# Value products of a retention kernel gathered into one stretch per batch

## What is computed

```
xn = layernorm(x)
x  = x + retention(xn; Wq, Wk, Wv, Wo) + ffn(xn)

retention, 8 heads of 16, chunk by chunk of the sequence:
    attn    = (q_c @ k_c.T) * D                 # D: decay below the diagonal
    o_intra = attn @ v_c
    o_inter = (q_c * decay_q) @ S
    S       = decay_s * S + (k_c * decay_k).T @ v_c
    o       = o_intra + o_inter                 # then o @ Wo

ffn:
    h = bitlinear(xn, w_fc) + gate * (xn @ v.T @ fast_b.T @ u.T)
    r = max(h, 0)
    out = bitlinear(r * r, w_proj)              # ternary weights times a row scale
```

## Time and profile before

| | before |
|---|---|
| three executions, us | 179.24, 181.82, 179.17 |
| span of the profiled execution, us | 177.4 |
| TensorE busy, us | 157.6 |
| VectorE busy, us | 137.3 |
| ScalarE busy, us | 78.8 |
| GpSimd busy, us | 61.0 |

### The profile page before, as it was taken

One profiled execution on the slowest core, in us unless ns is written; L12 is line 12 of the kernel. 1 busy time (PEld: TensorE's weight loads), 2 busy tenths in 40 slices (PEclk: granted clock), 3 DMA queues, 4 the chain that ended last, 5 costly groups with the idle time before them and its releaser, 6 DMA issues.

```text
span 177.4 us, 3389 instructions
## 1 busy us (share of the span) xinstructions
PE 157.6 (89%) x1177; PEld 122.1 (69%) x1177; DVE 137.3 (77%) x343; ACT 78.8 (44%) x155; POOL 61.0 (34%) x46
## 2 busy tenths in 40 slices
PE   1561298799999999999999999999999999999992
PEld 0240295577887788787878787878787877788771
DVE  6889898789867988788768876887789757764551
ACT  2510276471277316732583238423762177217710
POOL 8699700065005600380019000920074005500550
PEclk9999999999999999999999999999999999999998
DMA  4970041205240333024301521061005210431001
GB/s 156 431 299 0 0 64 56 59 4 81 37 124 0 60 60 118 0 43 75 114 5 26 92 73 45 7 104 60 6 0 89 33 59 0 74 48 61 0 4 59
DMA packets 7913, 11.65 MB, mean 66 GB/s; under 512 B 1296, under 2 KB 5520, under 8 KB 7776
## 3 DMA queue, kind: packets, MB, share of 16 engines
q1 hardware_dynamic: 7584, 10.82, 25.4%
q10 hardware_dynamic: 320, 0.72, 1.2%
HBM read 5.50 MB, written 2.10 MB: 43 GB/s over the span
## 4 chain that ended last, share of the span: by engine, by line
PE 81%; DVE 13%; DMA 2%; issue 1%; ACT 1%; DVEq 0%
PE ps_o L696 10%; PE ps_score L634 10%; PE ps_score L636 8%; PE ps_score L635 8%; PE ps_work L635 6%; PE ps_work L634 6%; PE ps_work L636 6%; PE ps_y L706 4%; PE ps_y L708 4%; DVE q_dec L453 4%; PE ps_o L685 4%; PE ps_state L688 3%; PE ps_work L656 3%; PE ps_work L630 2%; DMA x_in<-x_tok 2%; PE ps_work L657 2%
## 5 line engine op out<-in xcount | busy, mean ns | idle before, releaser
L301 POOL TENSOR_TENSOR sq_lo<-square,sq_hi 128x512 fp32r<-128x512 f32 x32 | 42.4, 1347 | 107.5 <-ACT sq_hi L369 106.7
L481 DVE TENSOR_TENSOR scores<-ps_score,cst 128x512 f32<-128x512 f32 x64 | 43.8, 686 | 12.6 <-PE ps_score L636 12.5
L365 ACT ACTIVATE square<-ps_work 128x512 f32<-128x512 f32 x32 | 19.0, 599 | 36.3 <-PE ps_work L636 35.6
L634 PE MATMUL ps_score<-q_exp,k_hi 128*128 128x512 f32 x64 | 28.3, 441 | 1.7 <-DVE scores L481 1.7
L636 PE MATMUL ps_score<-q_exp,k_lo 128*128 128x512 f32 x64 | 25.2, 394 | 0.0
L635 PE MATMUL ps_score<-q_exp,k_hi 128*128 128x512 f32 x64 | 25.1, 392 | 0.0
L696 PE MATMUL ps_o<-scores,v_pad 128*32 128x128 f32 x512 | 20.6, 279 | 0.0
L373 ACT ACTIVATE square<-square 128x512 f32<-128x512 f32 x32 | 19.2, 628 | 0.0
L369 ACT ACTIVATE sq_hi<-square 128x512 fp32r<-128x512 f32 x32 | 18.2, 621 | 0.0
L696 PEld LDWEIGHTS ps_o<-scores,v_pad 128*32 128x32 f32 x512 | 12.0, 109 | 7.7 <-issue 5.8
L634 PEld LDWEIGHTS ps_score<-q_exp,k_hi 128*128 128x128 f32 x64 | 12.1, 188 | 6.3 <-issue 3.0
(11 more groups left out here) (94 smaller groups left out, 315.8 us busy)
## 6 DMA issues: line engine op xcount, KB each, us to landing
q_exp<-q_parts SPq DMA_DIRECT2D x60, 64.0 KB, 2.3
x_in<-x_tok SPq DMA_DIRECT2D x8, 256.0 KB, 3.0
resid<-x_feat SPq DMA_DIRECT2D x1, 2048.0 KB, 10.8
out_feat<-resid SPq DMA_DIRECT2D x8, 256.0 KB, 2.1
ffn_in<-ffn_weights SPq DMA_DIRECT2D x1, 576.0 KB, 4.8
cst<-const ACTq DMA_DIRECT2D x1, 468.0 KB, 6.2
wqkv<-qkv_weights ACTq DMA_DIRECT2D x1, 192.0 KB, 5.1
rank_in<-rank_weights ACTq DMA_DIRECT2D x1, 41.1 KB, 2.8
```

Source lines behind the costliest of these rows:

```text
L301: nc.gpsimd.tensor_tensor(sq_lo[:, f, :], square[:, f, :], sq_hi[:, f, :].bitcast(F32), ALU.subtract).then_inc(lo_ready, 1)
L365: nc.scalar.activation(square[:, f, :], ps_work[f % 2][:], ACT.Relu).then_inc(relu_ready, 1)
L481: nc.vector.tensor_tensor(scores[c % 2][:, half * HALF:(half + 1) * HALF], ps_score[half][:].rearrange("p (h i) -> p h i", h=HALF), causal ...
L634: mm(out, w_hi, x_hi, start=True, stop=False)
```

## The change

The value products of the four chunks leave their four places and become one stretch of 32 matmuls, between `project_vk(nxt, 1)` and `second_product`. Its one wait is for all eight masks of the batch. The scores get four buffers, one per chunk. Only the state's product of chunk 1, now the first to write `ps_o` in a batch, carries the start flag; all others add or, where nothing was written since, overwrite.

```diff
-        scores = [sb(f"scores{p}", [P, H, CH]) for p in range(2)]
+        scores = [sb(f"scores{c}", [P, H, CH]) for c in range(NT)]
...
-                    scores[c % 2][:, half * HALF:(half + 1) * HALF],
+                    scores[c][:, half * HALF:(half + 1) * HALF],
...
-                       q_dec[b.parity][:, c * CH:(c + 1) * CH], start=True, stop=False)
+                       q_dec[b.parity][:, c * CH:(c + 1) * CH], start=(c == 1), stop=False,
+                       skip_group_check=True)
...
-            def own_values(b, c):
-
-                pe.wait_ge(scores_ready, b.count(2 * NT, 2 * c + 2))
-                for s in range(HEADS_IN_GROUP):
-                    for g in range(NG):
-                        ins = mm(ps_o[g * GW:(g + 1) * GW, c * CH:(c + 1) * CH],
-                                 v_pad[b.parity][:, c, g, s * GW:(s + 1) * GW],
-                                 scores[c % 2][:, g * HEADS_IN_GROUP + s, :],
-                                 start=(c == 0 and s == 0), stop=(s == HEADS_IN_GROUP - 1))
-                if c == NT - 1:
-                    ins.then_inc(o_done, 1)
+            def own_values(b):
+
+                pe.wait_ge(scores_ready, b.count(2 * NT, 2 * NT))
+                for c in range(NT):
+                    for s in range(HEADS_IN_GROUP):
+                        for g in range(NG):
+                            ins = mm(ps_o[g * GW:(g + 1) * GW, c * CH:(c + 1) * CH],
+                                     v_pad[b.parity][:, c, g, s * GW:(s + 1) * GW],
+                                     scores[c][:, g * HEADS_IN_GROUP + s, :],
+                                     start=False, stop=(s == HEADS_IN_GROUP - 1), skip_group_check=True)
+                ins.then_inc(o_done, 1)
...
                 score(b, 1, 1)
-                own_values(b, 0)
                 score(b, 2, 0)
                 if later > 0:
                     project_q(nxt, b)
                 carry(b, 1)
-                own_values(b, 1)
                 score(b, 2, 1)
...
                     project_k(nxt)
-                own_values(b, 2)
                 carry(b, 3)
-                own_values(b, 3)
                 if later > 0:
                     project_vk(nxt, 1)
+                own_values(b)
                 second_product(b, range(0, NF))
```

## The result

The change makes the kernel slower: 189.38 us in the median (187.86 to 189.59) against 179.20 in the same comparison, a ratio of 1.057 with a 95% interval of 1.049 to 1.066. The forecast was 190.7. The profiled execution has a span of 187.7 us against 177.4.

The account below looks back on a forecast made before the run. TensorE's program order was taken as the bound: +1.71 us in each of batches 0 to 6 (12.0), -0.35 in the last, taken as +11.45. Span 188.9 plus 1.84 gives 190.7; range 184.5 to 194 (0.82).

Parts of the forecast that it names:

- What goes away: On TensorE, four value stretches (3.04 us) become one of 2.08 with entering and leaving: 0.96 us saved a batch without waits.
- Query projection: TensorE after score (2,0): waits for the input's low part, ready at 110.00, and starts at 110.06, a wait of 0.11.
- Carry 2: TensorE after score (2,1): waits for VectorE's state 2, ending at 112.11, and starts at 112.17, a wait of 0.28.
- Low queries: VectorE's low part of the queries: could begin at 112.60, but GpSimd's subtraction keeps its end at 113.98.
- Score (3,1): TensorE waits for mask (2,1), behind the low queries: starts at 114.65, wait 0.64 plus 0.11 for restarting.
- Low keys: VectorE makes them after mask (3,1) and a small step; TensorE waits 1.49 before the second key/value projection, resuming at 117.85.
- Behind the stretch: TensorE after the value stretch: leaving and second product 1.97, output product 0.70, then the next batch at 123.30.
- Output product: No wait: the output's low part takes 1.46 from the stretch's end, under the 1.97 of the second product covering it.
- Last batch: No next batch, so no key wait: its value stretch ends at 171.0 against 171.34, a change of -0.35.
- the stretch did gain inside: Rival that the stretch gains nothing inside: 0.57 a chunk, 3.1 us more, 193.8; chance 0.08.
- GpSimd did hold VectorE: Rival that VectorE is not held by GpSimd: low keys 0.87 earlier a batch, 6.1 in all, 184.6; chance 0.10.
- keep the memory for two instructions: Rival that GpSimd's third subtraction follows its second at once: low keys about 1.15 later, 8.0 more, 198.7; chance 0.07.

Follow-up runs that it names:

- the bank: Eighth PSUM bank for the second key/value projection, which then needs no low-key wait: changed kernel 179.28 us, kernel before 178.59 us.
- The experiment on GpSimd: GpSimd's low-squares subtraction cut to 16 of 512 columns, the rest cleared once: changed kernel 186.42 us, kernel before 181.00 us.
- the first half: Against the kernel before, value products of chunks 0 and 1 in place, 2 and 3 one stretch behind the second key/value projection: 186.84 us.
- the version that beats both: Against the kernel before, chunks 0 and 1 in place, 2 and 3 one stretch behind the second key/value projection, plus eighth PSUM bank: 176.61 us.

## Why the prediction was right, point by point

- **What bounds the kernel**: right. TensorE's order is the time: the bank took away the key wait of 1.38 with its restart, and the batch fell by 1.46.
- **What goes away**: the pieces are right. A stretch of two chunks took 1.01 and one of four 1.88, against 0.44 + 0.57 = 1.01 and 1.89 in the sum.
- **Query projection**: a wait of 0.11 was forecast. The gap was 0.29 (115.80 + 0.23 = 116.03 to 116.32), since TensorE started 0.24 after the low part of the input (115.39 + 0.69 = 116.08) and not 0.06. Ahead of this projection it works off waits for three semaphores in turn; that this takes the extra time is only argued.
- **Carry 2**: forecast at 112.17 after a wait of 0.28, came at 112.15 (118.28 - 6.13). The later query projection had used the wait up.
- **Low queries**: forecast to end at 113.98 though they begin at 112.60; they ran from 112.59 to 113.95. The experiment on GpSimd shows why.
- **Score (3,1)**: forecast 114.65, came at 114.60, after a wait of 0.51 (from 120.10 + 0.12 = 120.22 to 120.73) instead of 0.64. That the two misses above hardly reach the sum isn't luck: this score starts when the mask behind the low queries is done, and GpSimd fixes that end, so what is waited for earlier is not waited for here.
- **Low keys**: this is the term that was mis-sized. Forecast from 117.10 to 117.79 and TensorE at 117.85; they started at 116.95, ran 0.68, and TensorE resumed at 117.69. Mask (3,1) came 0.05 earlier (122.42 - 6.13 = 116.29), VectorE passed on 0.60 after its start, where the sum went by its recorded end, and 0.06 after that of the small step instead of 0.08. A wait of 1.49 was forecast; from the carry's end at about 122.44 to 123.82 it was 1.38. The sum also put the wait down to VectorE's masks; ScalarE's high keys were as late (116.89), and in the first half the same path, 1.80 us long, gave the same wait with the early stretches in place.
- **Behind the stretch**: 2.63 instead of 2.67. With the 0.16 above this is the whole difference between the forecast 1.71 a batch and the measured 1.51; times seven 1.4 us.
- **Output product**: no wait, as forecast; the covers named there held.
- **Last batch**: forecast 0.35 shorter; 15.06 became 14.74 us from its first product to the final one, 0.32.
- **The sum**: forecast +11.45, measured 10.3 on the span.
- **Rivals**: the stretch did gain inside. GpSimd did hold VectorE; with it out of the way the low keys were forecast 0.87 earlier in the batch and came 0.68 earlier, where 0.16 is the term above. Inside the batches it did not keep the memory for two instructions, although its third subtraction was ready: that one stretched from 1.29 to 1.73, so VectorE was let in ahead of it. Ahead of batch 0 that does happen (the last section). The key wait did not come alone, though the first half shows what it does by itself. The clock stayed: products in the batches keep their 0.23.

## What to carry to other kernels

Before work is moved in a program order, look at what its old place covered: here two stretches of 0.57 us stood exactly between a product and the wait for its low part, and the row said so by starting the waiting product 0.14 after its releaser's end. Gathering like products is worth an entry and an exit each, but only inside the slack of the waits they leave behind. A lead given to an engine is worth nothing if that engine meets a neighbour's instruction that ends at the same time as before. Where a wait comes only from a shared buffer, one more buffer takes the reason for it away and nothing has to stand in front of it: the best version here moves the two stretches that the bank makes free to move and leaves alone the two that cover the masks.

## What the runs showed of the hardware

- Column-tiled value products in a row take 0.44 us a chunk of 16 records, and only the last pays 0.57: two chunks 1.01 us, three 1.44 (116.31 to 117.75), four 1.88.
- Inside the batches a VectorE subtraction of two SBUF operands that comes during a GpSimd subtraction ends 0.54 us after GpSimd's, whether it came 0.43 or 0.82 us before that end, and GpSimd's next one grows from 1.29 to 1.56 or 1.73. The 0.54 is less than the 0.69 that it takes alone.
- Ahead of batch 0 the same meeting comes out in two ways, and the starts of batch 0 lie 2.1 us apart, like the steps between executions (177.12 and 179.2). VectorE scales a weight (line 543) while GpSimd subtracts (12.95 to 14.22); a memset of 8192 columns stands ready behind that. The first two rows are from the kernel before, the third from the kernel with chunks 0 to 2 gathered:

```profile
13.12 8.05 DVE L543 TENSOR_SCALAR wo_scaled<-ffn_in,inv_scale 128x128 f32<-128x128 f32 x1
14.16 6.93 POOL L295 MEMSET q_exp<- 128x8192 f32 x1
...
13.11 1.19 DVE L543 TENSOR_SCALAR wo_scaled<-ffn_in,inv_scale 128x128 f32<-128x128 f32 x1
```

In the kernel before VectorE is passed over for a second instruction: it ends at 21.17, 0.08 after the memset, and batch 0 starts at 26.87. In the other VectorE gets in between, is held only by a later scaling (line 555, 16.80 to 22.62), and batch 0 starts at 24.73. During that memset a subtraction of two SBUF operands (line 547) took 0.67 as ever; it was VectorE's scalings that were held. The clearing in the small-subtraction runs is a second memset right behind the first (21.03 to 22.83); VectorE's row grew to 9.80, and batch 0 starts at 28.60. In the profiles of the kernel before with the bank (its execution took 182.43 us) and of the first half (189.33 us) the constants landed late, TensorE waited over 5 us for them, and batch 0 starts at 29.46 and 29.45. These are profiles of different kernels, which are alike ahead of batch 0 but for the bank and the clearing; no execution of 177 us was profiled. Why one execution comes out one way and the next another stays open.

- TensorE's clock. Here is how batch 0 begins with chunks 0 to 2 gathered:

```profile
24.73 0.79 PE L634 MATMUL ps_work<-xn_hi,w_hi 128*128 128x512 f32 x1 [4.29 <-DVE k_tok L477]
```

The mean granted clock from 25 to 30 us is 0.54, near the lower level of 1.2 GHz, behind this wait of 4.29 us, and products of 512 columns start 0.43 apart, against 0.23 in the batches. This execution took 180.03 us, others of the same kernel 181.12 and 181.28: of the 2 us of its early start it kept little more than 1. In the kernel before the products ahead of batch 0 take 0.43 as well (11.51 to 11.94), though the record reads the upper level there, as in the earlier trace rows. In the profile of the version that beats both it reads 0.50 from 21.2 to 25.5 us, and its products there start within 0.01 us of those of the kernel before. So a record at the upper level didn't always mean it; I go by the starts. In none of the profiles did the clock fall behind the waits of up to 1.4 us inside the batches, by the record or by the starts.
